# First P tile ordered by the arrival of K's parts, second u product inside it, first magnitude earlier, K's second half updated in pairs

## The reference

```python
x = x + _L0_ffn_ref(_L0_cond_ref(x, thresholds, deltas, zeropoints), router_w, A, B)
x = x + _L1_ffn_ref(_L1_cond_ref(x, itok, W, lora_A, lora_B_w), gate, kernel, bias, ...)

# _L0_cond_ref: each element is quantised with the step and zero point of the first of
# 8 groups whose threshold its magnitude stays under, and zero above all of them
gi = jnp.sum(jnp.abs(x)[..., None] <= thresholds, axis=-1)
x_quant = jnp.clip(jnp.round(x / d) + zp, 0, N_LEVELS - 1)
# _L0_ffn_ref: 4 experts of rank 16, the best 2 by router logits, softmax gates
delta = jnp.einsum('te,teo->to', gates, all_deltas)
# _L1_cond_ref: x @ W.T plus a rank 32 adapter chosen per batch
# _L1_ffn_ref: x @ kernel + bias plus two rank 32 adapters
```

## Time and profile before

| | us |
|---|---|
| median of 3 runs | 448.9 (448.44 to 449.27) |
| profiled execution, its time | 446.5 |
| profiled execution, its span | 444.7 |
| PE busy | 433.0 |
| DVE busy | 382.2 |
| ACT busy | 363.0 |
| POOL busy | 54.2 |

### The profile page before, as it was taken

One profiled execution on the slowest core, in us unless ns is written; L12 is line 12 of the kernel. 1 busy time (PEld: TensorE's weight loads), 2 busy tenths in 40 slices (PEclk: granted clock), 3 DMA queues, 4 the chain that ended last, 5 costly groups with the idle time before them and its releaser, 6 DMA issues.

```text
span 444.7 us, 5682 instructions
## 1 busy us (share of the span) xinstructions
PE 433.0 (97%) x2152; PEld 343.7 (77%) x2152; DVE 382.2 (86%) x386; ACT 363.0 (82%) x314; POOL 54.2 (12%) x55
## 2 busy tenths in 40 slices
PE   8989999999999999999999999999999999999996
PEld 8857777878788888768677778788778868877873
DVE  1696979999899989999999899989998999899400
ACT  1579999965697999999899989989999989897002
POOL 0000003000021000200401200322521200401000
PEclk9989999999999999999999999999999999999999
DMA  7999439950459965360772863783872930361304
GB/s 275 360 315 410 125 86 288 215 144 1 118 167 294 238 169 226 68 164 1 168 152 47 197 171 49 178 189 48 177 191 47 207 67 14 55 136 21 75 0 94
DMA packets 40173, 66.09 MB, mean 149 GB/s; under 512 B 26994, under 2 KB 27250, under 8 KB 37874
## 3 DMA queue, kind: packets, MB, share of 16 engines
q0 software_dynamic: 8368, 38.28, 36.4%
q1 hardware_dynamic: 31778, 27.45, 21.1%
HBM read 55.23 MB, written 18.87 MB: 167 GB/s over the span
## 4 chain that ended last, share of the span: by engine, by line
PE 59%; ACT 17%; DVE 10%; issue 7%; DMA 5%; SPq 1%; ACTq 0%; DVEq 0%
PE bank L1198 13%; PE bank L1200 12%; PE bank L1199 12%; ACT val L483 6%; PE bank L1172 6%; PE bank L1057 5%; ACT level L470 4%; DVE val L762 3%; DMA wst<-w_in 3%; DMA ab_raw<-ab_in 2%; DVE val L744 2%; PE bank L1081 2%; PE bank L1097 1%; PE bank L1096 1%; PE bank L1132 1%
## 5 line engine op out<-in xcount | busy, mean ns | idle before, releaser
L762 DVE COPY_PREDICATED val<-inside,val 128x2048 f32<-128x2048 uint8 x56 | 142.5, 2545 | 0.3
L483 ACT ACTIVATE val<-level,shift,small 128x2048 f32<-128x2048 int16 x64 | 133.9, 2092 | 6.3 <-PE bank L1057 6.3
L470 ACT ACTIVATE level<-xq,inv 128x2048 int16<-128x2048 f32 x64 | 127.8, 1998 | 0.5
L1198 PE MATMUL bank<-p_hi,x_hi 128*128 128x512 f32 x256 | 106.9, 417 | 0.0
L1200 PE MATMUL bank<-p_hi,x_lo 128*128 128x512 f32 x256 | 100.1, 391 | 0.0
L1199 PE MATMUL bank<-p_lo,x_hi 128*128 128x512 f32 x256 | 100.0, 391 | 0.0
L744 DVE TENSOR_SCALAR val<-val,width,unshift 128x2048 f32<-128x2048 f32 x64 | 85.9, 1342 | 3.5 <-ACT val L483 3.3
L753 DVE TENSOR_SCALAR inside<-absx,thr 128x2048 uint8<-128x2048 f32 x56 | 72.1, 1288 | 0.0
L1198 PEld LDWEIGHTS bank<-p_hi,x_hi 128*128 128x128 f32 x256 | 48.1, 188 | 13.7 <-issue 4.6
L1199 PEld LDWEIGHTS bank<-p_lo,x_hi 128*128 128x128 f32 x256 | 48.1, 188 | 11.3 <-issue 2.6
L1200 PEld LDWEIGHTS bank<-p_hi,x_lo 128*128 128x128 f32 x256 | 48.1, 188 | 10.4
(11 more groups left out here) (111 smaller groups left out, 492.9 us busy)
## 6 DMA issues: line engine op xcount, KB each, us to landing
out_t<-bias_in POOLq DMA_DIRECT2D x8, 1024.0 KB, 16.1
out_t<-ost POOLq DMA_DIRECT2D x15, 512.0 KB, 7.1
wst<-w_in SPq DMA_DIRECT2D x14, 512.0 KB, 7.0
xq<-xt_in POOLq DMA_DIRECT2D x7, 1024.0 KB, 8.2
x_hi<-xt_in POOLq DMA_DIRECT2D x7, 1024.0 KB, 6.3
x_lo<-xt_in POOLq DMA_DIRECT2D x14, 512.0 KB, 7.0
la<-la_in SPq DMA_DIRECT2D x4, 512.0 KB, 5.5
kst<-k_in SPq DMA_DIRECT2D x4, 512.0 KB, 13.1
```

Of the source, the lines that this page charges most:

```text
L470: nc.scalar.activation(level[:, g % 2], xq[:, c % 2], ACT.Copy, scale=inv[:, group(g)]).then_inc(levels_made, 1)
L483: nc.scalar.activation(val[:, turn(c, g)], level[:, g % 2], ACT.Relu, bias=shift[:, group(g)], scale=par[:, 1, group(g)]).then_inc(raised, 1)
L762: nc.vector.copy_predicated(val[:, acc(c)], inside[:, g % 2], val[:, turn(c, g)]).then_inc(merged, 1)
L1198: mm(o, x_hi[b % 3][:, k, at], p_hi[:, h, k], start=k == 0 and n < OWN, stop=False)
```

## The change

It has four parts.

1. **The first P tile** has its own function. It takes the two products that need only `kp_hi`, part by part as they come, then four of the `kp_lo` products, then the whole of `u_product(1)`, then the identity and the other four. The first half's banks are dealt out anew (`kfirst` begins with `obank[0]`), and two of PE's waits on `k_sum` go from 1 and 2 to 2 and 3.
2. **ACT** makes `magnitude(0)` right after the first `raise_levels`, ahead of `weight_hi(1)`. **DVE** puts `mask(0, 2)` and `weight_lo(2)` between `value(0, 1)` and `merge(0, 1)`.
3. **K's second half** follows the table `K_AT`: parts 3 and 4 after tile 4, parts 5 and 6 after tile 5, part 7 after tile 6. Before, part 5 came after tile 6, part 6 ahead of the router product of step 7, and part 7 inside tile 7. DVE adds them at the start of the following step. The waits of the parts follow the two banks, so that part 4, not part 6, waits for `t_made`.
4. **The lists.** One quantisation group fewer in step 5 and one more in step 8; batch 0's `gate` one step later.

```diff
-    kfirst = [obank[1], obank[2], obank[3], sbank[1], zbank, obank[0]]
+    kfirst = [obank[0], obank[1], obank[2], obank[3], sbank[1], zbank]
-    kbank = [[kfirst[o % len(kfirst)] for o in range(KT)], [zbank if o == KT - 2 else sbank[1] for o in range(KT)]]
+    kbank = [kfirst + [obank[1], obank[2]], [zbank if o in (4, 6) else sbank[1] for o in range(KT)]]
...
-    LAGS = [(3, 4, 6, 7, 9, 10), ...
-    TAKEN = [0, 1, 1, 2, 2, 2, 1, 1, 0, 1, 1, 1, 1, 1, 1, 1, 1, 2]
+    LAGS = [(3, 4, 6, 8, 9, 10), ...
+    TAKEN = [0, 1, 1, 2, 2, 1, 1, 1, 1, 1, 1, 1, 1, 1, 1, 1, 1, 2]
...
+    K_AT = {1: (0,), 2: (1,), 3: (2,), 4: (3, 4), 5: (5, 6), 6: (7,)}
...
             raise_levels(0, 0)
+            magnitude(0)
             act.wait_ge(bwp_made, 1)
             weight_hi(1)
...
-            magnitude(0)
             levels(0, 1)
...
             mask(0, 1)
-            quant(0, 1)
+            value(0, 1)
+            mask(0, 2)
+            weight_lo(2)
+            merge(0, 1)
...
             for n in range(STEPS):
-                if 1 < n < KT:
-                    k_add(1, n - 2)
+                for o in K_AT.get(n - 1, ()):
+                    k_add(1, o)
                 if n == KT:
-                    k_add(1, KT - 1)
                     kp_lo_part(1)
...
-                if n == KT - 1:
-                    k_add(1, n - 1)
...
                 if h == 0 and o >= len(kfirst):
-                    pe.wait_ge(k_sum, o - len(kfirst) + 1)
+                    pe.wait_ge(k_sum, o - len(kfirst) + 2)
...
+                elif h and o == 4:
+                    pe.wait_ge(t_made, HALVES * NG)
                 elif h:
-                    pe.wait_ge(t_made, HALVES * NG)
+                    pe.wait_ge(k_sum, KT + (o if o < 4 else o - 1))
...
+            def first_tile():
+
+                pe.wait_ge(w_lo_made, 1)
+                for o in range(KT):
+                    pe.wait_ge(kp_hi_made, o + 1)
+                    mm(obank[0], w_hi[0][:, o], kp_hi[:, o], start=o == 0, stop=False)
+                    mm(obank[0], w_lo[0][:, o], kp_hi[:, o], start=False, stop=False)
+                for o in range(KT):
+                    if o == KT // 2:
+                        u_product(1)
+                        pe.wait_ge(ident_made, 1)
+                        mm(obank[0][:, 0:P], ident, ident, start=False, stop=False)
+                    pe.wait_ge(kp_lo_made, o + 1)
+                    last = mm(obank[0], w_hi[0][:, o], kp_lo[:, o], start=False, stop=o == KT - 1)
+                last.then_inc(ofull, 1)
```

More of the change, by code:

```diff
@@ L223, in build @@
     AHEAD, HOLD = 2, 1
[L224 to L225 removed]
+    LAGS = [(3, 4, 6, 8, 9, 10), (3, 4, 5, 5, 5, 6), (2, 4, 4, 6, 7, 8), (2, 3, 3, 4, 4, 6), (2, 4, 5, 6, 7, 8), (2, 3, 4, 5, 6, 8), (1, 2, 2, 4, 5, 6), (2, 2, 2, 2, 4, 5)]
+    TAKEN = [0, 1, 1, 2, 2, 1, 1, 1, 1, 1, 1, 1, 1, 1, 1, 1, 1, 2]
     ORDER = [(c, g) for c in range(BATCH) for g in range(G)]
@@ L926, in _ @@
             for n in range(STEPS):
-                if 1 < n < KT:
-                    k_add(1, n - 2)
+                for o in K_AT.get(n - 1, ()):
+                    k_add(1, o)
                 if n == KT:
-                    k_add(1, KT - 1)
                     kp_lo_part(1)
-                if n and n + 1 < STEPS and n + 1 not in (KT, KT + 1):
+                if n > 1 and n + 1 < STEPS and n + 1 not in (KT, KT + 1):
                     weight_lo(load_of(n + 1))
@@ L981, in k_update @@
                     pe.wait_ge(k_sum, KT)
-                elif h and o == KT - 1:
-                    pe.wait_ge(k_sum, KT + o - 1)
-                elif h and o < KT - 2:
-                    pe.wait_ge(k_sum, KT + o)
+                elif h and o == 4:
+                    pe.wait_ge(t_made, HALVES * NG)
                 elif h:
-                    pe.wait_ge(t_made, HALVES * NG)
+                    pe.wait_ge(k_sum, KT + (o if o < 4 else o - 1))
                 mm(kbank[h][o], ab[:, 0, o * P:(o + 1) * P], ab[:, 1, h * HALF:(h + 1) * HALF],
@@ L1115, in _ @@
                 if n < KT - 1:
-                    u_product(n)
+                    if n != 1:
+                        u_product(n)
                     if n:
@@ L1121, in _ @@
                             k_update(0, k)
-                if n == KT - 1:
-                    k_update(1, n - 1)
                 if h == 0 and n in MID:
                     mid(MID[n])
-                pe.wait_ge(w_lo_made, load_of(n) + 1)
-                if n >= RING:
-                    pe.wait_ge(ofree, n - RING + 1)
-                for o in range(KT):
-                    if n % KT == 0:
-                        pe.wait_ge(kp_lo_made, h * KT + o + 1)
-                    mm(obank[n % RING], w_hi[side(n)][:, o], kp_hi[:, o], start=o == 0, stop=False)
-                    mm(obank[n % RING], w_hi[side(n)][:, o], kp_lo[:, o], start=False, stop=False)
-                    if o == KT - 2 and i * P // HALF == h:
-                        pe.wait_ge(ident_made, 1)
-                        mm(obank[n % RING][:, i * P % HALF:i * P % HALF + P], ident, ident, start=False, stop=False)
-                    last = mm(obank[n % RING], w_lo[side(n)][:, o], kp_hi[:, o], start=False, stop=o == KT - 1)
-                    if n == KT - 1 and o < KT - 1:
-                        last.then_inc(kp_read, 1)
-                    if n == KT - 1 and o == KT - 2:
-                        k_update(1, n)
-                last.then_inc(ofull, 1)
+                if n == 0:
+                    first_tile()
+                else:
+                    pe.wait_ge(w_lo_made, load_of(n) + 1)
+                    if n >= RING:
+                        pe.wait_ge(ofree, n - RING + 1)
+                    for o in range(KT):
+                        if n == KT:
+                            pe.wait_ge(kp_lo_made, h * KT + o + 1)
+                        mm(obank[n % RING], w_hi[side(n)][:, o], kp_hi[:, o], start=o == 0, stop=False)
+                        mm(obank[n % RING], w_hi[side(n)][:, o], kp_lo[:, o], start=False, stop=False)
+                        if o == KT - 2 and i * P // HALF == h:
+                            pe.wait_ge(ident_made, 1)
+                            mm(obank[n % RING][:, i * P % HALF:i * P % HALF + P], ident, ident, start=False, stop=False)
+                        last = mm(obank[n % RING], w_lo[side(n)][:, o], kp_hi[:, o], start=False, stop=o == KT - 1)
+                        if n == KT - 1 and o < KT - 1:
+                            last.then_inc(kp_read, 1)
+                    last.then_inc(ofull, 1)
                 if n == 0:
@@ L1150, in _ @@
                     u_adapters(n)
-                if 0 < n < KT - 1:
-                    k_update(1, n - 1)
+                for o in K_AT.get(n, ()):
+                    k_update(1, o)
                 if n in V_AT:
```

1 line of the change is left out of this document (removed).

## The result

The changed kernel takes **443.53 us** (median of 4 runs, 443.02 to 444.00) where the kernel before takes 448.67 (4 runs, 448.22 to 449.27; 448.22 is new beside the three that gave 448.9 above). The ratio is 0.988, with a 95% interval of 0.987 to 0.990. The profiled execution took 443.02 us with a span of 441.2. Against the 446.5 and 444.7 of before's profiled execution this is 3.5 us less, where the sum said 3.7. This compares one execution with one: other profiled executions of before, further down, have spans of 443.9 to 447.4.

The account below looks back on a forecast made before the run. The prediction took PE to bound the third stage, PE and ACT the second, with DVE deciding its end. DVE's 3.8 us less 0.1 gave 3.7 off 446.5, 442.8; plus 2.4 to the median, 445.2 us, range 443.6 to 448.3.

Parts of the forecast that it names:

- the sum: Whole kernel: third stage entered 3.7 us earlier, giving 442.8 profiled; the median, 2.4 us higher, gives 445.2.
- DVE's count: Eighth W tile to the second stage's end: DVE's work, 58.2 us, puts the last `weight_lo` at 153.3, 3.8 us earlier.
- PE's first tile: Start of second stage: no wait before the pairs, full clock, tile and second u product done at 31.7 us.
- the prediction's own bound on its landing: W's tile 1, first tile: landed at 26.9, in time by 0.3 us or up to 0.7 us late.
- term of 3.85 us: PE's gain at the first tile: 0.3 us earlier with the u product of 3.56 us already done.
- ACT 2.2 us ahead: Behind the first tile: 1.9 us from `absx` in idle time, 0.3 from PE's earlier results, kept through step 4.
- all behind it: Everything after 75 us, said to be wrong if ACT is not 2.2 us ahead there.
- K's second half: Before the router product and tile 8: earlier sums by DVE remove PE's waits of 1.15 and 0.56 us.
- The moved group: DVE behind the eighth W tile: landing at 94.0, `weight_lo(7)` at 95.05, then 5.0 us more work for DVE.
- The clock term: First tile's matmuls: half clock behind PE's idle wait cost 1.7 us, counted as full gain.
- The rival "no change": Up to 75 us: PE runs into full ACT, whose idle times prove needed; 448.7 us, chance 0.10.

Follow-up runs that it names:

- Parts 3 and 4 alone: Kernel before with only K's second half by the new table and the two new lists: 445.69 us, ratio 0.995.
- the wait put in: Changed kernel with PE made to wait, ahead of batch 0's router product, for DVE's last update of K: 453.78 us, ratio 1.010.
- late loads on purpose: Kernel before with the 272 KB load of ra issued ahead of ab's instead of last: 449.13 us, ratio 1.000; changed kernel likewise: 443.81 us.
- parts 2 to 4: Changed kernel with the first tile and second u product as in the kernel before: 445.09 us, ratio 0.993.
- part 1 alone: Kernel before with only the new first tile, its banks and the wait on `k_sum`: 448.83 us, ratio 1.002.
- part 2: Kernel before with only `absx` earlier on ACT and the new order on DVE: 446.48 us, ratio 0.997.

## Why the prediction was right and wrong

**The direction was right, and so was the mechanism in its main line: PE gets to the third stage earlier by what DVE's count gave, with two terms at the start too large.** Step by step:

- *PE's first tile*: pairs from 22.65 to 26.3 (22.60 to 26.24), the u product at 27.2 or up to 0.7 later (27.78), PEclk 1.00 (1.00). The tile and product end at 32.38 in place of 31.7, of which 0.5 us is the wait for W's tile 1; the prediction's own bound on its landing had this case in it. The adapters and tables behind take 0.3 us longer than in before (2.2 against 1.9). So the term of 3.85 us was too large: 2.9 are there at tile 1.
- *ACT 2.2 us ahead*: 1.3. The idle time in front of `w_hi` was filled as said, but PE's results let `ust` and `tst` start 0.4 and 0.5 us later than in before and not 0.3 us earlier. This is PE's late tile again. The text had called a wrong lead here fatal for "all behind it". It was not: at the eighth W tile ACT and DVE wait for a transfer anyway.
- *K's second half*: the waits of 1.15 and 0.56 us are gone, a wait of 0.4 us came in ahead of the v product. Parts 3 and 4 alone give 1.9 us of span.
- *The moved group*: the W tile was issued at 83.16, 1.0 us earlier and not 2.1, and the fills at 67.04, 1.3 earlier and not 2.1. Yet it landed nearly when forecast, for it took 11.0 us from its issue where it had taken 11.9. That is partly luck, since the times in between were 11.4 and 10.9 in two other profiles of the changed kernel. Its rounding begins at 94.22 (94.0), `weight_lo(7)` at 95.32 (95.05), the last one at 153.71 (153.3), PE's wait at the end of the stage 0.67 (0.6). DVE's count gave the third stage 3.7 us earlier, and it came 3.5 earlier. DVE's count from the landing to the last `weight_lo` held within 0.2 us (58.4 for 58.2). The 3.5 us of the profiles, being a difference of two single executions, agree with it partly by luck too: the lowest times differ by 3.0.

**The step that failed** is the last sentence of the Sum: "the runs' median is 2.4 us higher, 448.9, and gives 445.2". It carries before's distance between median and profile over to the changed kernel. The changed kernel's distance is 0.5 us (443.53 against 443.02). With 442.8 + 0.5 the forecast would have been 443.3, within 0.2 of the result. The distance of 2.4 us was no constant that both kernels share. In part it was chance: before's 135 later executions have a median of 448.0, 1.5 us above the profiled 446.5. The rest is time that executions of before lose in spread: the median of the 135 lies 2.3 us above their lowest, that of the changed kernel only 0.7 to 1.1. The best times tell the profile's story, 445.7 us the lowest of before and 442.7 of the changed kernel, 3.0 us; the medians of the pairs here differ by 4.1 to 5.1.

**What the distance was made of.** Shown: in 37 of 135 executions of before the clock is lower, and they are 2.8 us longer. Filling the wait of 1.15 us ahead of the router product all but ends them (none and one of 12, for 8 of 23 in before on that chip). Without these 37 the median of the 135 would be 447.4 in place of 448.0, so that they make 0.6 us of the distance. The prediction priced this wait at its 1.15 us alone. That the fall then lasts through the router product, as in the profile with the wait put in, is argued from that profile, since none of before's caught one. Still open: the rest of the spread, and so the larger part of the step that failed. Filling the wait lowered the median by 0.2 us only, and late loads on purpose did not raise it, so why before's other executions lie 1.7 us above its lowest (447.4 for 445.7) and the changed kernel's 0.7 to 1.1 isn't settled. The four profiles tie it to ACT's wait for the last W tile; no experiment here moved that wait alone.

**The clock term** in the first tile (1.7 us, taken as full gain) was right as a difference on PE but wrong as a price. Filled alone it brought nothing, since the transfers of the adapters and tables stood behind it. In the changed kernel, whose u product covers these transfers, putting the wait back goes with some 1.6 us beyond the wait in the executions of lower clock. The Trainium skill, "TensorE: Matmul & The Clock Gate", Part 1, has half clock as the default that activity lifts; before's trace and that of the wait put in agree, with 0.50 behind 2.07 and 4.64 us without work, and those in which these waits are gone, with 1.00. The profiles of parts 2 to 4 show besides that the clock can stay at 1.00 behind 1.9 to 2.1 us.

**The parts don't add up.** Alone they give no gain (first tile, ratio 1.002), 1.1 (`absx` and DVE's order, by the medians) and 1.9 us (K and lists, by the medians and the profile); the first tile gives some 1.6 only with the others. The rival "no change" was right for part 1 alone, and nearly for the reason that it named: PE ran into ACT's order by way of DVE, whose `w_lo` for tile 2 came 1.78 us late behind an `absx` that ACT still made at 35.88.

## What to carry to other kernels

A profile is one execution: before adding the distance to the median to a forecast, ask what that distance is, and take it from more than one profile and three runs. If the list of executions shows different mean clocks, try filling PE's idle times one by one, as here that of 1.15 us: such a wait can cost the half clock behind it too, in some of the executions. A stall taken from one engine may pay only when those next in line (here ACT and DVE) are moved too: try the parts together before dropping one that shows nothing alone.

## What was not expected of the hardware

- The same idle time takes the clock down in some executions only. Ahead of the first tile all four profiles of before have a stretch at 0.50 behind their 2.07 us, and those of part 2, of parts 3 and 4, of parts 2 to 4 and of before with late loads have 1.00 behind 1.91 to 2.07. With the wait put back into the changed kernel, 9 of 12 executions show 0.994 to 0.996 over all and three show 1.0.
- The fall can come at a later and shorter idle time. With late loads the kernel before waited 2.01 us, kept 1.00 in its first tile, waited 1.45 us for the adapters' transfer and had 0.50 after that:

```profile
35.00:36.00 1.00, 1.00 (x3) 0.25 (x2) 0.00 (x0) 0.29 (x1) 0.00 (x0) 0.50 1.03 386
```

- A W tile of 512 KB lands 3.7 us after its issue with the output's fills held back, and 11.0 us where four of them (1 MB each) were issued 16 us ahead of it, by another engine. In the two traces the fills are what made it late; the prediction had left that undecided.
